# Heads: the output weights applied to the scaled sums as one f32 matmul for each half

## The reference

```python
def _L0_attn_ref(x, weight):
    b, t, c = x.shape
    nh = NUM_HEADS            # 16
    hs = c // nh              # 8
    y = x.reshape(b, t, nh, hs).transpose(0, 2, 1, 3)
    scores = jnp.einsum('bhtk,bhsk->bhts', y, y) / math.sqrt(hs)
    attn = jax.nn.softmax(scores, axis=-1)
    o = jnp.einsum('bhts,bsc->bhtc', attn, x)
    o = o.transpose(0, 2, 1, 3).reshape(b, t, nh * c)
    return o @ weight         # (16*128) x 128
```

## Time and profile before

| | |
|---|---|
| median of 3 runs | 2653.85 us (2650.99 to 2660.51) |
| the profiled execution's own time | 2655.64 us |
| its span, first to last instruction | 2653.9 us |
| mean granted clock of TensorE, share of 2.4 GHz | 0.978 |
| TensorE busy, matmuls and weight loads | 2509.9 us (95%) and 1894.6 us (71%) |
| VectorE, ScalarE, POOL busy | 2161.6 us (81%), 1826.5 us (69%), 1206.7 us (45%) |
| the attention layer in question, from its first matmul to its last sum | 599.6 to 1614.0 us |

### The profile page before, as it was taken

How to read it: one execution, slowest core, us unless ns; L and a number is a source line. 1 busy time by engine, 2 the same in 40 slices (tenths; PEclk the granted TensorE clock), 3 DMA queues, 4 the chain that set the end, 5 groups by cost and what they waited for, 6 DMA issues and landing times. The chain is left out here.

```text
span 2653.9 us, 34843 instructions
## 1 busy us (share of the span) xinstructions
PE 2509.9 (95%) x11075; PEld 1894.6 (71%) x11075; DVE 2161.6 (81%) x2866; ACT 1826.5 (69%) x3038; POOL 1206.7 (45%) x1252
## 2 busy tenths in 40 slices
PE   7999999996999999999999998999999998788888
PEld 4788888873777777777777765788888886566556
DVE  6777777776999999999999997877777775578665
ACT  4555555556999999999999995555555555567676
POOL 3666666663322323232332323566666662154401
PEclk9999999998999999999999999999999999889999
DMA  3666666645433434344343431666666640000000
GB/s 98 143 139 139 139 139 142 144 88 167 109 107 101 108 104 112 104 105 103 107 109 104 107 93 47 133 144 142 142 142 142 144 105 8 25 25 9 9 6 35
DMA packets 106520, 269.89 MB, mean 102 GB/s; under 512 B 30688, under 2 KB 35552, under 8 KB 106208
## 3 DMA queue, kind: packets, MB, share of 16 engines
q1 hardware_dynamic: 81328, 233.84, 36.8%
q0 software_dynamic: 24576, 33.62, 5.3%
q10 hardware_dynamic: 432, 0.20, 0.0%
HBM read 256.78 MB, written 10.76 MB: 101 GB/s over the span
## 5 line engine op out<-in xcount | busy, mean ns | idle before, releaser
L675 POOL TENSOR_TENSOR moe_e_lo<-moe_e_hidden,moe_e_hi 128x512 fp32r<-128x512 f32 x512 | 661.1, 1291 | 332.7 <-ACT moe_e_hi L627 332.5
L632 ACT ACTIVATE psum<-psum 128x512 f32<-128x512 f32 x512 | 297.8, 582 | 473.8 <-PE psum L90 473.7
L952 DVE TENSOR_TENSOR heads_e_lo<-heads_e,heads_e_hi 128x2048 fp32r<-128x2048 f32 x256 | 586.5, 2291 | 29.1 <-ACT heads_e_hi L902 24.2
L789 POOL DMA_DIRECT2D heads_left<-heads_parts x512 | 296.0, 599 | 652.8 <-PE psum L843 592.9
L895 ACT ACTIVATE heads_e<-psum 128x1024 f32<-128x1024 f32 x512 | 520.2, 1023 | 77.9 <-PE psum L843 77.8
L652 DVE TENSOR_TENSOR moe_weighted<-moe_spread,psum 128x512 f32<-128x512 f32 x512 | 351.2, 686 | 185.6 <-PE psum L90 181.4
L88 PE MATMUL psum<-heads_e_hi,heads_v_lo 128*128 128x512 f32 x1024 | 425.6, 416 | 1.1 <-DVE heads_u L921 1.1
L89 PE MATMUL psum<-heads_e_lo,heads_v_hi 128*128 128x512 f32 x1024 | 403.1, 394 | 0.0
L90 PE MATMUL psum<-heads_e_hi,heads_v_hi 128*128 128x512 f32 x1024 | 400.9, 391 | 0.0
L88 PE MATMUL psum<-moe_n_hi,moe_w_lo 128*128 128x512 f32 x1024 | 398.8, 389 | 2.1 <-ACT moe_route_mask L458 1.3
L90 PE MATMUL psum<-moe_n_hi,moe_w_hi 128*128 128x512 f32 x1024 | 398.4, 389 | 0.0
(11 more groups left out here) (403 smaller groups left out, 4031.9 us busy)
## 6 DMA issues: line engine op xcount, KB each, us to landing
moe_spread<-moe_mask SPq DMA_DIRECT2D x128, 1024.0 KB, 9.9
heads_right<-heads_parts SPq DMA_DIRECT2D x512, 64.0 KB
heads_left<-heads_parts POOLq DMA_DIRECT2D x512, 64.0 KB, 3.8
heads_scale<-heads_inverse_copy SPq DMA_DIRECT2D x64, 512.0 KB, 3.6
moe_raw<-in_gate SPq DMA_DIRECT2D x16, 256.0 KB, 11.6
moe_raw<-in_up SPq DMA_DIRECT2D x16, 256.0 KB, 11.7
moe_raw<-in_down SPq DMA_DIRECT2D x16, 256.0 KB, 11.7
heads_parts<-heads_e_hi SPq DMA_DIRECT2D x16, 256.0 KB, 3.2
```

Of the source, the lines that this page charges most:

```text
L632: act.activation(gate, gate, ACT.Silu).then_inc(self.silu_ready, 1)
L675: pool.tensor_tensor(self.lo[:, p, :], self.hidden[:, p % 2, :], f(self.hi[:, p, :]), ALU.subtract).then_inc(self.low_ready, 1)
L789: eng.dma_start(f(tile[row:row + 2 * HEAD, h % 2, :]), parts_dram[dims, order:order + 2, at]).then_inc(loaded[h % 2], 16)
L952: dve.tensor_tensor(e_lo[:, s:s + 2, :], e[:, s % 4:s % 4 + 2, :], f(e_hi[:, s:s + 2, :]), ALU.subtract).then_inc(low, 1)
```

## The change

The weights `w` stay one f32 tile, loaded by the norm at the same place in SP's queue, without POOL's split. `u` becomes f32 with two buffers; `u_hi`, `u_lo`, the functions that made them and their semaphores are gone. `add_head` waits for `scaled_ready` and makes one f32 matmul for each half, with the f32 weights and `u`. `scale_sums` waits until the weights of the head before the last have been applied, since it now writes the buffer from which they read.

```diff
@@ -731,7 +731,7 @@
 
     with ExitStack() as ctx:
         sb, sem = sb_in(ctx, nc), sems_in(ctx, nc, tag)
-        w_hi, w_lo = sb(f"{tag}_w_hi", [P, HEADS * P], F32R), sb(f"{tag}_w_lo", [P, HEADS * P], F32R)
+        w = sb(f"{tag}_w", [P, HEADS * P])
         e_hi, e_lo = sb(f"{tag}_e_hi", [P, TILES, T], F32R), sb(f"{tag}_e_lo", [P, TILES, T], F32R)
         row_hi = e_hi[:, 0:BATCH, :].rearrange("p a b -> p (a b)")
         row_lo = e_lo[:, 0:BATCH, :].rearrange("p a b -> p (a b)")
@@ -742,7 +742,7 @@
         copied = [sem(f"copied{b}") for b in range(BATCH)]
         BATCH_COPIED = 16 * 3 * HALVES
         layernorm(nc, f"{tag}_norm", psum, consts, x, row_hi, row_lo,
-                  splits=[(dram["head_w"], w_hi[:, :], w_lo[:, :])], copies=[(parts_dram[:, 0, :], 0), (parts_dram[:, 1, :], 1), (parts_dram[:, 2, :], 0)],
+                  loads=[(w[:, :], dram["head_w"])], copies=[(parts_dram[:, 0, :], 0), (parts_dram[:, 1, :], 1), (parts_dram[:, 2, :], 0)],
                   copied=copied)
 
         left = sb(f"{tag}_left", [P, 2, T], F32R)
@@ -753,8 +753,7 @@
         inverse = sb(f"{tag}_inverse", [P, 2, 32])
         inverse_rows = sb(f"{tag}_inverse_rows", [P, 2, 32])
         scale = sb(f"{tag}_scale", [P, 2, T])
-        u = sb(f"{tag}_u", [P, HALVES, BANK])
-        u_hi, u_lo = sb(f"{tag}_u_hi", [P, 2, HALVES, BANK], F32R), sb(f"{tag}_u_lo", [P, 2, HALVES, BANK], F32R)
+        u = sb(f"{tag}_u", [P, 2, HALVES, BANK])
         SCORES, OUT, SUM = 0, 4, 6
 
         left_loaded, right_loaded = ([sem(f"{side}_{parity}") for parity in ("even", "odd")] for side in ("left", "right"))
@@ -764,7 +763,7 @@
         divided, inverse_ready, inverse_stored = sem("divided"), sem("inverse"), sem("inverse_stored")
         cleared = sem("cleared")
         scale_loaded = [sem("scale_even"), sem("scale_odd")]
-        out_done, scaled_ready, u_high, u_low = sem("out"), sem("scaled"), sem("u_high"), sem("u_low")
+        out_done, scaled_ready = sem("out"), sem("scaled")
         sum_done, added = sem("sum_done"), sem("added")
         HEAD_LOADS = 8
         ACT_HIGH = (1, 3, 5, 7)
@@ -821,13 +820,12 @@
                 def add_head(g):
 
                     cols = slice(g % HEADS * P, (g % HEADS + 1) * P)
-                    pe.wait_ge(u_low, (g + 1) * HALVES)
+                    pe.wait_ge(scaled_ready, (g + 1) * HALVES)
                     if g % HEADS == 0:
                         after(pe, added, g // HEADS * HALVES)
                     for half in range(HALVES):
-                        last = product(pe, psum[:, SUM + half, :], (w_hi[:, cols], w_lo[:, cols]),
-                                       (u_hi[:, g % 2, half, :], u_lo[:, g % 2, half, :]),
-                                       first=g % HEADS == 0, last=g % HEADS == HEADS - 1)
+                        last = pe.matmul(psum[:, SUM + half, :], w[:, cols], u[:, g % 2, half, :], start=g % HEADS == 0,
+                                         stop=g % HEADS == HEADS - 1, skip_group_check=True)
                     last.then_inc(sum_done, 1)
 
                 def scores(h, s):
@@ -878,12 +876,6 @@
 
             @block.scalar
             def _(act):
-                def u_highs(g):
-                    after(act, sum_done, g - 1)
-                    for half in range(HALVES):
-                        act.wait_ge(scaled_ready, g * HALVES + half + 1)
-                        act.copy(u_hi[:, g % 2, half, :], u[:, half, :]).then_inc(u_high, 1)
-
                 for k in range(0, 2 * VALUE_BANKS, 2):
                     act.wait_ge(turned, k + 1)
                     act.copy(turned_value(k), psum[:, k % 8, :]).then_inc(v_by_act, 1)
@@ -900,9 +892,6 @@
                         if n < BATCH:
                             act.wait_ge(copied[n], BATCH_COPIED)
                         act.copy(e_hi[:, s, :], e[:, s % 4, :]).then_inc(act_high, 1)
-                    if s == TILES - 1 and h >= 1:
-                        u_highs(h - 1)
-                u_highs(COUNT - 1)
 
             @block.vector
             def _(dve):
@@ -916,16 +905,10 @@
                 def scale_sums(g):
                     dve.wait_ge(scale_loaded[g % 2], 16 * (g // 2 + 1))
                     dve.wait_ge(out_done, (g + 1) * TILES)
+                    after(dve, sum_done, g - 1)
                     for half in range(HALVES):
-                        after(dve, u_low, (g - 1) * HALVES + half + 1)
-                        dve.tensor_tensor(u[:, half, :], scale[:, g % 2, half * BANK:(half + 1) * BANK],
+                        dve.tensor_tensor(u[:, g % 2, half, :], scale[:, g % 2, half * BANK:(half + 1) * BANK],
                                           psum[:, OUT + half, :], ALU.mult).then_inc(scaled_ready, 1)
-
-                def u_lows(g):
-                    for half in range(HALVES):
-                        dve.wait_ge(u_high, g * HALVES + half + 1)
-                        dve.tensor_tensor(u_lo[:, g % 2, half, :], u[:, half, :], f(u_hi[:, g % 2, half, :]),
-                                          ALU.subtract).then_inc(u_low, 1)
 
                 def add_batch(b):
                     dve.wait_ge(sum_done, (b + 1) * HEADS)
@@ -953,12 +936,9 @@
                                       ALU.subtract).then_inc(low, 1)
                     if s == TILES - 2:
                         invert(h)
-                    if s == TILES - 2 and h >= 1:
-                        u_lows(h - 1)
                     if s == 2 and h > HEADS and h % HEADS == 2:
                         add_batch(h // HEADS - 1)
                 scale_sums(COUNT - 1)
-                u_lows(COUNT - 1)
                 add_batch(BATCH - 1)
                 dve.wait_ge(added, BATCH * HALVES)
```

## The result

The changed kernel took 2676.59 us in the median of 4 runs (2671.51 to 2680.45), the kernel before 2654.26 us in the 4 runs beside it: ratio 1.0071, interval [1.0054, 1.0088]. Two later comparisons of the same two kernels gave 1.0044 [1.0027, 1.0060] and 1.0049 [1.0032, 1.0066]. Over all runs the changed kernel's mean is 2671.0 us (16 runs) and that of the kernel before 2657.7 us (51 runs): 13.3 us, 0.5% slower. Forecast were 16.4 us more; the medians of the first comparison differ by 22.3 us.

The account below looks back on a forecast made before the run. The prediction took TensorE's stream to bound the loop. On a median of 2653.85 us, +20.5 (applied weights) - 3.0 (norm) - 1.1 (tail) = +16.4 us gave 2670.2 us, range 2661 to 2680.

Parts of the forecast that it names:

- What bounds the kernel: In the loop over heads TensorE's stream is the time; VectorE and ScalarE fit into it with little room.
- The applied weights: In `add_head`, two f32 matmuls (1.716 us) replace six fp32r ones (1.39 us): +0.33 us a head, +20.5 us over 62.
- The norm: At the stage's head, dropping POOL's split frees VectorE's first cast, so the heads start earlier: -3.0 us.
- the hold of 0.4 us by the third chunk: In the norm, the third chunk's low part, ready near 613.1, holds SP's copies some 0.4 us.
- The tail: After the loop, the last two heads' weights end at 1611.61 instead of 1612.68: -1.1 us.
- The sum: Loop, norm and tail together: +16.4 us on the median, 2670.2 us, 0.6% slower; chance 0.66.
- Rival (b): At the stage's start, more gain (-4.1 us) or a kind clock (-1.5): +13.2 us, 2667.1 us; chance 0.17.
- (a): In the applied weights, each f32 matmul costs four full fp32r passes: +28.7 us in the loop, 2678.5 us; chance 0.10.
- (c): In the loop, VectorE is the real pace, so dropping its subtractions saves 78 us: about 2572 us; chance 0.04.
- (d): In the applied weights, each f32 piece takes one pass: -0.47 us a head, 2620.6 us; chance 0.03.

Follow-up runs that it names:

- four products: The kernel before with a fourth fp32r matmul, low part with low part, in each half of the applied weights; 2687.01 us, ratio 1.0114.
- the parts made: The changed kernel with ScalarE's casts and VectorE's subtractions of the scaled sums still made, their results unused; 2661.37 us in one time.

## Why the prediction was right

**What bounds the kernel** held: TensorE paces the loop. Taking some 2.5 us a head from the other engines changed nothing, adding 0.46 us of matmuls added 0.42. The weight loads' busy share of 71% was no sign of room.

**The applied weights** were forecast at +0.33 us a head and measured at +0.285: 62 x 0.285 = 17.7 us for 20.5. This is the term that was mis-sized. The f32 matmuls cost what was said (0.86 us). What I had not seen is that the products behind them go a little quicker in this place: from 1012.88 to the next scores at 1015.47 are 2.59 us, where before 2.63 passed (1010.16 to 1012.79):

```profile
1010.16 0.39 PE L89 MATMUL psum<-heads_e_lo,heads_v_hi 128*128 128x512 f32 x1
```

In the medians over the loop it is 2.60 for 2.63: the last eight steps of the pair are 0.227 us each, where they averaged 0.231. That is 0.03 of the missing 0.04 us; the rest is rounding. The same quickening stands behind the applied weights in the run with four products and in the one with the parts made, and is absent with the f32 matmuls doubled. It isn't ScalarE's and VectorE's work for the parts. Nor is it the change's own: in the kernel before, one of the three other pairs of a head ends in steps of 0.227 us and takes 3.39 us where the others take 3.42; in the changed kernel's second profile two do, and its head takes 15.29 us. What starts it stays open.

**The norm**: forecast -3.0, measured -3.5 (38.3 to 34.8) and, against the repeated profiles, -3.4. The mechanism was shown by putting the split back. Two steps were off. Counted from the first squares, the first copy leaves 3.8 us earlier (12.1 to 8.3), not 3.3, and the hold of 0.4 us by the third chunk didn't lengthen SP's copies: from the first copy to the first load of a head are 14.9 us in both. And the first scores no longer wait for those loads last:

```profile
634.87 0.50 PE L841 MATMUL psum<-heads_right,heads_left 32*128 32x512 f32 x4 [0.83 <-DVE heads_v_lo L923]
```

In all three profiles of the changed kernel VectorE's last copy of the transposed x comes last, and in the second one of the kernel before too. It stands behind the same barrier as the loads, so the gain came through by either path.

**The tail**: forecast -1.1. The rows before, and the last scores of the changed kernel:

```profile
1595.14 0.51 PE L843 MATMUL psum<-heads_right,heads_left 32*128 32x512 f32 x4
...
1612.72 1.29 DVE L934 TENSOR_TENSOR x<-x,psum 128x512 f32<-128x512 f32 x2 [1.74 <-PE psum L90]
```

```profile
1608.09 0.51 PE L841 MATMUL psum<-heads_right,heads_left 32*128 32x512 f32 x4
```

From the last score group to the sum into x it took 1612.72 - 1595.14 = 17.58 us, and takes 1624.88 - 1608.09 = 16.79; this holds one application inside the loop, 0.29 us longer, so the tail gained 1.08.

**The sum**: 17.7 - 3.4 - 1.1 = 13.2 us by the measured terms, 12.1 in the stage, 13.3 between the means of all runs; 16.4 were forecast. The stage falls a little short of the terms because the first profile of the kernel before has one head of 15.83 us and the second of the changed kernel has heads of 15.29. The first comparison's 22.3 us looks like a miss the other way, but lies 9 us above the difference of the means; in its profile 6.3 us go with a lower granted clock in the decayed attention, whose code the change doesn't touch. So the forecast lies 5.9 us under the one number and 3.1 over the other, and on which side a median of four runs fell was luck. The loop's pace, the price of the f32 matmul, the split and the tail were foreseen; the quicker steps were not. Rival (b) named nearly the number of the means, +13.2, but by a gain of 4.1 us and a kind clock at the start; its clock was the right suspect in the wrong place: I looked for it in the 40 us at the start of the stage, and it was in the decayed attention. Rivals (a), (c) and (d) fell to the runs above.

## What to carry to other kernels

Before trading several cheap matmuls for one dear one, find out which engine's starts make the rhythm: if it is TensorE's, freeing the others is worth nothing, and 0.86 us for an f32 matmul of 512 columns stands against 0.69 for three fp32r ones. Look for the gain in the prologue instead: a large POOL instruction beside a chain of short VectorE ones can hold one of them for its whole length, and engines idle at the end of the same stage can take it over. And when a small difference is measured, compare marks of the changed stage between profiles; the medians of four runs were off by 9 us here.

## What the runs showed of the hardware that was not expected

The granted clock of an unchanged stage differed between executions (0.83 to 0.87 in the decayed attention, which took 232.4 to 240.9 us), and whole runs of one kernel at a mean clock of 0.973 and 0.977 lie 11 us apart, almost as much as the change. In the norm every VectorE cast that began under an instruction of POOL ended 0.28 or 0.29 us after it, whether that one took 1.27 or 4.52 us. And fp32r matmuls of 512 columns step at 0.227 or 0.231 us in the same loop, by something that none of these runs took hold of; eight such steps a head made 2 of the 20 us of the main term.
